# Cross attentions of a fused decoder: pairs of heads on TensorE, three score banks, a shared bank pair for front units and tail

## The chip, the cores and the metric

One core of one Trainium2 chip runs the whole program. The metric is the device time of one execution in microseconds (us), lower is better. The core's engines are TensorE (PE; PEld is its weight load), VectorE (DVE), ScalarE (ACT), GpSimd (POOL) and SyncE (SP, which issues the DMAs). Each runs its own list of instructions in order; they meet through semaphores.

## The reference

Two decoder layers for 16 sequences of 112 tokens with 256 features, in fp32. Each layer has a self attention, a cross attention over 375 context tokens and a feed-forward part, each followed by a residual and a layernorm. The change touches the two cross attentions only (the kernel's stages cross0 and cross1, one function):

```python
Q = split_heads(x @ W_q); K = split_heads(ctx @ W_k); V = split_heads(ctx @ W_v)  # 16 heads of 16
scores = einsum('bhqd,bhkd->bhqk', Q, K) / sqrt(16)      # 112 x 375 a head
scores = where(mask == 0, -1e9, scores)
X = einsum('bhqk,bhkd->bhqd', softmax(scores), V)
x = layernorm(x + merge_heads(X) @ W_o)
```

## The kernel before, in words

`stage_cross_attention` (L395) treats one sequence (a "batch") after another, 16 in each of the two stages; batches 1 to 12 run in a loop of two, the rest are written out (`over_batches`, L475). Within a batch 16 places i = 0..15 follow each other, one a head, and each engine has its own hand-written list of what it does at which place.

For a head h:
- TensorE, `scores` (L685): one matmul, 96 stacked rows, 376 keys, into one of two PSUM banks (h % 2); waits for the maximum of h - 2, which read that bank.
- VectorE, `maximum` (L889): adds the mask, scales, and takes the minimum of the negated scores (L893).
- ScalarE, `exponent` (L799): exponent and row sum (L803), into one of 8 buffers.
- TensorE, `turn` (L694), three places later (TL = 3): three 112 x 125 transposes (L699) into one of two banks; waits for the exponent of h and for the evacuation of h - 2.
- `evacuate`: even heads VectorE (L900), odd heads ScalarE (L809), both at three places' lag (EL = 3).
- TensorE, `values` (L703), for four heads: 24 small matmuls (L712) into bank 6 (OUT).

Two kinds of work are threaded between the heads. The **front units** make the operands of later batches, each in bank u % 2 of the first two: V0, V1, V2 (values, L669, of the next batch; VectorE adds the bias, L871), C0, C1 (context transposes, L664; ScalarE copies, L787), Q (queries, 8 matmuls, L674; ScalarE makes the high part, L791, VectorE the low part, L878), K0, K1 (keys, L681; L796, L883). After them SP stores the parts to DRAM and loads them back stacked, for the batch after the next. The **tail** finishes the batch before, all in bank 7: part 0 ScalarE copies the summed values to osb (L815) and TensorE turns them (L720), VectorE divides by the row sums into otok (L907); part 1 TensorE turns otok (L725), ScalarE copies it to o (L818); part 2 the output product (L731) and VectorE's chain y, variance (L910 to L915); part 3 xn (L919), its transposes (L737) and ScalarE's copy into xt (L821). POOL computes the reciprocal root (L635) and stores x (L637).

The places, by engine (a comment line names the engine; the lists of VectorE and ScalarE are not in the diff except for their banks):

```python
# TensorE: scores(i); turn(i - 3); front; tail; values
TAIL_AT = {6: 0, 8: 1, 10: 2, 14: 3}
FRONT_AT = {2: V0, 4: V1, 6: V2, 7: C0, 8: C1, 10: Q, 12: K0, 14: K1}
VALUES_AT, VALUES_OF_LAST = {8: 0, 12: 1}, {0: 2, 4: 3}
# ScalarE: tail 0; evacuate(i - 3) at even i; exponent(i); front; tail 1, 2
TAIL_AT = {5: 0, 9: 1, 15: 2}
FRONT_AT = {7: C0, 8: C1, 10: Q, 12: K0, 14: K1}
# VectorE: maximum(i); front; tail; evacuate(i - 3) at odd i
TAIL_AT = {7: 0, 11: 1, 13: 2}
FRONT_AT = {5: V0, 6: V1, 7: V2, 11: Q, 13: K0, 15: K1}
```

Each unit on TensorE waits until the reader of the unit two before it is done (`wait_front_read`, L500). The first batch has no tail, the last but one only V units, the last none. Before batch 0 a prologue runs C0, C1, Q, K0, K1 and then all eight units.

## Time and profile before

| | |
|---|---|
| median of 3 runs | 2669.48 us (2666.8 to 2669.84) |
| profiled execution | 2664.71 us, its span 2663.0 us |
| mean granted clock of TensorE over the span | 0.948 |
| PE / PEld / DVE / ACT / POOL busy over the span | 88 / 69 / 65 / 51 / 20 % |
| cross0, all of it | about 150 to 559 us |
| cross1, all of it | about 1305 to 1712 us |
| a middle batch | 306.13 / 13 = 23.55 us |

A matmul's record runs from its start to a modelled end and overlaps the next one's; what a step costs is the time from its start to the start of the next. "[0.40 <-DVE cross_pt L900]" behind a row is the idle time before it and who ended it. An "xN" row merges N instructions.

### The profile page before, as it was taken

The page shows a single profiled execution, that of the slowest core. Times are in us where ns is not written, and L with a number is a line of the kernel's source. Part 1 is how long each engine was busy: PE and PEld are TensorE (multiplying, and loading weights), DVE is VectorE, ACT ScalarE, POOL GpSimd, SP SyncE. Part 2 cuts the span into 40 slices and gives each one's busy share as a digit, 9 for nine tenths or more (in the row PEclk, how much of TensorE's full clock was granted, in tenths as well). Part 3 has the DMA queues.
Part 4 walks back from the last instruction along what each step waited for, and adds up shares of the span by engine and source line. Part 5 has one row for each costly group of instructions (what it writes and reads, how often), then busy time and mean ns, then how long its engine had stood idle before and what let it go on. Part 6 is the DMA issues. An engine that isn't in the chain of part 4 may idle for free. (4 is left out here: it accounts for less than half of the span.)

```text
span 2663.0 us, 51055 instructions
## 1 busy us (share of the span) xinstructions
PE 2346.0 (88%) x15551; PEld 1834.5 (69%) x15551; DVE 1735.1 (65%) x4497; ACT 1357.5 (51%) x3657; POOL 526.4 (20%) x623
## 2 busy tenths in 40 slices
PE   5769999977999968888599999589999999999995
PEld 3547777766999955555377777467777777777762
DVE  1336666763888755666376677546676676767678
ACT  2236666743666515555276666465444444444430
POOL 3010000023000140000100000054343343434321
PEclk8879999978999979999799999889999999999998
DMA  5046655413666420000366665010010100101000
GB/s 161 0 120 130 123 119 119 102 50 112 203 210 208 150 63 1 0 0 0 90 133 122 129 125 124 25 52 17 20 37 2 36 17 22 36 1 37 1 1 28
DMA packets 191015, 194.92 MB, mean 73 GB/s; under 512 B 55457, under 2 KB 182642, under 8 KB 190834
## 3 DMA queue, kind: packets, MB, share of 16 engines
q1 hardware_dynamic: 187762, 185.36, 27.7%
q0 software_dynamic: 3072, 7.34, 0.9%
q8 instruction: 90, 1.47, 0.2%
q14 instruction: 91, 0.75, 0.1%
HBM read 144.23 MB, written 48.43 MB: 72 GB/s over the span
## 5 line engine op out<-in xcount | busy, mean ns | idle before, releaser
L803 ACT ACTIVATE cross_pr<-cross_sc,cross_mn 112x375 f32<-112x375 f32 x512 | 310.5, 607 | 230.6 <-DVE cross_mn L893 229.6
L2317 ACT ACTIVATE switch_vt<-switch_ps,switch_chosen 112x128 f32<-112x128 f32 x1024 | 290.8, 369 | 267.0 <-PE switch_ps L105 256.5
L2391 DVE SCALAR_TENSOR_TENSOR all_x<-switch_ps,switch_go,all_x 112x256 f32<-112x256 f32 x512 | 245.6, 480 | 219.7 <-PE switch_ps L105 214.4
L893 DVE CUSTOM_DVE_ANT_0 cross_sc<-cross_ps,cross_masked 112x375 f32<-112x375 f32 x512 | 273.0, 543 | 176.4 <-PE cross_ps L691 155.3
L699 PE MATMUL cross_ps<-all_ident,cross_pr 112*125 112x112 f32 x1536 | 255.4, 275 | 23.6 <-DVE cross_pt L900 22.0
L699 PEld LDWEIGHTS cross_ps<-all_ident,cross_pr 112*125 112x125 f32 x1536 | 233.0, 189 | 45.3 <-DVE cross_pt L900 27.8
L2182 POOL TENSOR_TENSOR switch_v_halves<-switch_vt 112x512 f32<-112x512 f32 x128 | 164.8, 1287 | 484.3 <-ACT switch_vt L2317 484.1
L2391 DVE SCALAR_TENSOR_TENSOR switchgates_x_odd<-switch_ps,switch_go,switchgates_x_odd 112x256 f32<-112x256 f32 x512 | 243.2, 475 | 0.0
L691 PE MATMUL cross_ps<-cross_k,cross_q 96*112 96x376 f32 x512 | 222.0, 434 | 14.2 <-DMA cross_k<-cross_k_dram 11.1
L103 PE MATMUL switch_ps<-switch_ow,switch_cth 128*112 128x512 f32 x512 | 208.8, 408 | 12.5 <-DVE switchgates_x_odd L2391 12.1
L103 PE MATMUL switch_ps<-switch_vw,switchgates_xh 128*112 128x512 f32 x512 | 208.0, 406 | 7.9 <-DVE switch_vw L2376 7.9
L104 PE MATMUL switch_ps<-switch_vw,switchgates_xh 128*112 128x512 f32 x512 | 202.7, 396 | 0.0
L105 PE MATMUL switch_ps<-switch_vw,switchgates_xl 128*112 128x512 f32 x512 | 202.6, 396 | 0.0
L105 PE MATMUL switch_ps<-switch_ow,switch_ctl 128*112 128x512 f32 x512 | 201.6, 394 | 0.0
L104 PE MATMUL switch_ps<-switch_ow,switch_cth 128*112 128x512 f32 x512 | 201.5, 394 | 0.0
L635 POOL TENSOR_TENSOR cross_rstd<-cross_var,cross_half 112x1 f32<-112x1 f32 x32 | 17.4, 543 | 633.2 <-DVE cross_var L915 633.2
L103 PEld LDWEIGHTS switch_ps<-switch_ow,switch_cth 128*112 128x112 f32 x512 | 89.3, 174 | 70.1 <-DVE switchgates_x_odd L2391 44.7
L103 PE MATMUL experts_ps<-experts_xh,experts_w 128*128 128x256 f32 (+1 forms) x400 | 126.1, 315 | 12.2 <-ACT experts_h L1776 5.5
L900 DVE COPY cross_pt<-cross_ps 125x336 f32<-125x336 f32 x256 | 128.2, 501 | 1.6 <-PE cross_ps L699 1.5
L1776 ACT ACTIVATE experts_h<-experts_ps,experts_b1c 128x256 f32<-128x256 f32 x168 | 79.9, 475 | 86.5 <-PE experts_ps L105 83.8
L2185 POOL TENSOR_TENSOR switch_v_quarters<-switch_v_halves 112x256 f32<-112x256 f32 x128 | 122.0, 953 | 10.1
L103 PE MATMUL experts_ps<-experts_hh,experts_w 128*128 128x256 f32 (+1 forms) x400 | 122.5, 306 | 0.9 <-issue 0.6
(352 smaller groups left out, 5482.0 us busy)
## 6 DMA issues: line engine op xcount, KB each, us to landing
experts_w_raw<-in_L_ffn_w_dram SPq DMA_DIRECT2D x42, 1024.0 KB, 5.2
cross_k<-cross_k_dram SPq DMA_DIRECT2D x96, 375.0 KB, 8.0
cross_k_dram<-cross_ks SPq DMA_DIRECT2D x32, 750.0 KB, 4.6
cross_cx_raw<-in_ctx_dram SPq DMA_DIRECT2D x32, 375.0 KB
cross_q<-cross_q_dram SPq DMA_DIRECT2D x192, 56.0 KB, 4.4
switch_raw<-in_L_ffn_v_w_dram SPq DMA_DIRECT2D x16, 512.0 KB
switch_raw<-in_L_ffn_o_w_dram SPq DMA_DIRECT2D x8, 1024.0 KB, 5.5
cross_q_dram<-cross_qs SPq DMA_DIRECT2D x32, 224.0 KB, 3.6
```

The source lines that it names most:

```text
L103: nc.tensor.matmul(out, w[0], x[0], start=first, stop=False)
L104: nc.tensor.matmul(out, w[0], x[1], start=False, stop=False)
L105: return nc.tensor.matmul(out, w[1], x[0], start=False, stop=last)
L691: nc.tensor.matmul(ps[0:T, SCORES + h % 2, 0:KEYS], q[parity][:, h // 2, h % 2, :], kk[parity][:, h // 2, :], start=True, stop=True).then_ ...
L699: last = nc.tensor.transpose(ps[0:KP, TURNED + h % 2, t * T:(t + 1) * T], pr[:, h % NB, t * KP:(t + 1) * KP], ident[0:T, 0:T])
L803: nc.scalar.activation(pr[:, h % NB, :], sc[:, h % NB, :], ACT.Exp, bias=mn[parity][:, h:h + 1], scale=-1.0, accum_out=rs[parity][:, h:h + ...
L893: nc.vector.tensor_tensor_reduce(out=sc[:, h % NB, :], in0=ps[0:T, SCORES + h % 2, 0:S2], in1=mask_of[:], scale=-0.25, scalar=3e38, op0=AL ...
L900: nc.vector.tensor_copy(pt[:, h % NB, :], ps[0:KP, TURNED + h % 2, 0:KT * T]).then_inc(pt_dve, 1)
L2182: pool.tensor_tensor(v_halves[:], vt[:, b % 2, 0:E // 2, :], vt[:, b % 2, E // 2:E, :], ALU.add)\
L2185: pool.tensor_tensor(v_quarters[:], v_halves[:, 0:E // 4, :], v_halves[:, E // 4:E // 2, :], ALU.add)\
L2317: last = nc.scalar.activation(vt[:, b % 2, n * EH + e, :], ps[0:T, VALUES + n, e * PW:(e + 1) * PW], ACT.Copy, scale=chosen[parity][:, b, ...
L2391: nc.vector.scalar_tensor_tensor(out=total[:, b, :], in0=ps[0:T, OUTPUTS + n % 2, i * D:(i + 1) * D], scalar=go[:, b, e:e + 1], in1=total[ ...
```

## The change

On TensorE the places are taken in pairs: scores of i and i + 1, then turnings i - 3 and i - 2, and then for each place its tail part, its front unit and its values, in that order. C1, Q, K0 and K1 go one place later (9, 11, 13, 15), tail part 0 one place earlier (5). The scores have three banks (2, 3, 4), in the order 0, 1, 2, ... with bank 1 again for head 15; turned heads use banks 5 and 6, the values bank 7. The tail no longer has a bank of its own: parts 0 and 3 use front bank 0, parts 1 and 2 front bank 1. Front bank 0 holds V0, C0, C1, Q; bank 1 holds V1, V2, K0, K1. So the waits of TensorE are new: V0 for Q's reader, V1 for K1's, V2 for V1's, K1 for K0's, C1 for C0's, Q for C1's, C0 for V0's and for otok, K0 for V2's and for the variance, tail part 0 for V0's, part 1 for V2's, part 3 for Q's. The lists of VectorE, ScalarE, POOL and SP keep their order; only bank numbers change there.

```diff
@@ -439,7 +439,9 @@
         rstd = s.sb("rstd", [T, 1])
         xn = s.sb("xn", [T, D])
         ps = s.banks("ps", 8)
-        FRONT, SCORES, TURNED, OUT, TAIL = 0, 2, 4, 6, 7
+        FRONT, SCORES, TURNED, OUT = 0, 2, 5, 7
+        SCORE_BANKS = (0, 1, 2, 0, 1, 2, 0, 1, 2, 0, 1, 2, 0, 1, 2, 1)
+        TAIL_BANK = (0, 1, 1, 0)
 
         dve_passed, sp_passed, pool_passed = s.sem("dve_passed"), s.sem("sp_passed"), s.sem("pool_passed")
         w_loaded, const_loaded, w_turned, w_ready = (s.sem(n) for n in ("w_loaded", "const_loaded", "w_turned", "w_ready"))
@@ -486,7 +488,10 @@
             return {"last": (), "last but one": (V0, V1, V2)}.get(kind, tuple(range(UNITS)))
 
         def bank_of(u):
-            return (FIRST_UNITS + u) % 2
+            return {V0: 0, V1: 1, V2: 1, C0: 0, C1: 0, Q: 0, K0: 1, K1: 1}[u]
+
+        def score_bank(h):
+            return SCORES + SCORE_BANKS[h % H]
 
         def done_count(g, u):
             return g * UNITS + FIRST_UNITS + u + 1
@@ -498,12 +503,6 @@
             return g * DVE_UNITS + FIRST_DVE + DVE_ORDER[u]
 
         def wait_front_read(engine, g, u):
-            if u < 0:
-                g, u = g - 1, u + UNITS
-            if isinstance(g, int) and g < 0 and u < C0:
-                return
-            if isinstance(g, int) and g < -1:
-                return
             if u in (C0, C1):
                 engine.wait_ge(f_act, act_count(g, u))
             else:
@@ -652,10 +651,26 @@
                     last.then_inc(w_turned, 1)
             pe.wait_ge(w_ready, sum(transposed))
 
-            def front(g, parity, u):
+            def front(g, parity, u, tails=True):
+
 
                 bank = ps[:, FRONT + bank_of(u), :]
-                wait_front_read(pe, g, u - 2)
+                if u in (V0, V1):
+                    wait_front_read(pe, g - 1, Q if u == V0 else K1)
+                elif u in (V2, K1):
+                    wait_front_read(pe, g, u - 1)
+                elif u in (C1, Q):
+                    wait_front_read(pe, g, u - 1)
+                elif isinstance(g, int) and g < 0:
+                    pass
+                elif u == C0:
+                    wait_front_read(pe, g, V0)
+                    if tails:
+                        wait(pe, otok_ready, g - 1)
+                elif u == K0:
+                    wait_front_read(pe, g, V2)
+                    if tails:
+                        wait(pe, var_ready, g - 1)
                 if u in (C0, C1):
                     c = u - C0
                     if u == C0:
@@ -687,8 +702,9 @@
                     wait_front_read(pe, b, V2)
                     pe.wait_ge(q_stacked, (b + 1) * Q_PARTS * 16)
                     pe.wait_ge(k_stacked, (b + 1) * K_PARTS * 16)
-                wait(pe, s_max, b * H + h - 1)
-                nc.tensor.matmul(ps[0:T, SCORES + h % 2, 0:KEYS], q[parity][:, h // 2, h % 2, :],
+                taken = max((i for i in range(h - H, h) if score_bank(i) == score_bank(h)))
+                wait(pe, s_max, b * H + taken + 1)
+                nc.tensor.matmul(ps[0:T, score_bank(h), 0:KEYS], q[parity][:, h // 2, h % 2, :],
                                  kk[parity][:, h // 2, :], start=True, stop=True).then_inc(s_done, 1)
 
             def turn(b, h):
@@ -713,55 +729,66 @@
                                                 pt[:, h % NB, t * T:(t + 1) * T], start=t == 0, stop=t == KT - 1)
                 last.then_inc(pv_done, 1)
 
-            def tail(b, part):
+            def tail(b, part, units=()):
+
+                bank = ps[:, FRONT + TAIL_BANK[part], :]
                 if part == 0:
+                    if V0 in units:
+                        wait_front_read(pe, b + 2, V0)
                     pe.wait_ge(o_read, b + 1)
                     for g in range(4):
-                        last = nc.tensor.transpose(ps[0:T, TAIL, g * P:(g + 1) * P], osb[:, g * T:(g + 1) * T], ident[:])
+                        last = nc.tensor.transpose(bank[0:T, g * P:(g + 1) * P], osb[:, g * T:(g + 1) * T], ident[:])
                     last.then_inc(t1_done, 1)
                 elif part == 1:
+                    if V2 in units:
+                        wait_front_read(pe, b + 2, V2)
                     pe.wait_ge(otok_ready, b + 1)
                     for k in range(DC):
-                        last = nc.tensor.transpose(ps[:, TAIL, k * T:(k + 1) * T],
+                        last = nc.tensor.transpose(bank[:, k * T:(k + 1) * T],
                                                    otok[:, k * 8:(k + 1) * 8, :].rearrange("p a b -> p (a b)"), ident[0:T, 0:T])
                     last.then_inc(t2_done, 1)
                 elif part == 2:
                     pe.wait_ge(o_ready, b + 1)
                     for k in range(DC):
-                        last = nc.tensor.matmul(ps[0:T, TAIL, 0:D], o[:, k, :], w[OW][:, k, :],
+                        last = nc.tensor.matmul(bank[0:T, 0:D], o[:, k, :], w[OW][:, k, :],
                                                 start=k == 0, stop=k == DC - 1)
                     last.then_inc(y_done, 1)
                 else:
+                    if Q in units:
+                        wait_front_read(pe, b + 2, Q)
                     pe.wait_ge(xn_ready, b + 1)
                     for k in range(DC):
-                        last = nc.tensor.transpose(ps[:, TAIL, k * T:(k + 1) * T], xn[:, k * P:(k + 1) * P], ident[0:T, 0:T])
+                        last = nc.tensor.transpose(bank[:, k * T:(k + 1) * T], xn[:, k * P:(k + 1) * P], ident[0:T, 0:T])
                     last.then_inc(xt_done, 1)
 
-            TAIL_AT = {6: 0, 8: 1, 10: 2, 14: 3}
-            FRONT_AT = {2: V0, 4: V1, 6: V2, 7: C0, 8: C1, 10: Q, 12: K0, 14: K1}
+            TAIL_AT = {5: 0, 8: 1, 10: 2, 14: 3}
+            FRONT_AT = {2: V0, 4: V1, 6: V2, 7: C0, 9: C1, 11: Q, 13: K0, 15: K1}
 
             def batch(b, parity, kind):
                 first, units = kind == "first", units_of(kind)
-                for i in range(H):
-                    scores(b, parity, i)
-                    if i >= TL:
-                        turn(b, i - TL)
-                    elif not first:
-                        turn(b - 1, i - TL + H)
-                    if FRONT_AT.get(i) in units:
-                        u = FRONT_AT[i]
-                        front(b + 1, 1 - parity if u in (V0, V1, V2) else parity, u)
-                    if not first and i in TAIL_AT:
-                        tail(b - 1, TAIL_AT[i])
-                    if i in VALUES_AT:
-                        values(b, parity, VALUES_AT[i])
-                    elif i in VALUES_OF_LAST and not first:
-                        values(b - 1, 1 - parity, VALUES_OF_LAST[i])
+                for pair in range(0, H, 2):
+                    for i in (pair, pair + 1):
+                        scores(b, parity, i)
+                    for i in (pair, pair + 1):
+                        if i >= TL:
+                            turn(b, i - TL)
+                        elif not first:
+                            turn(b - 1, i - TL + H)
+                    for i in (pair, pair + 1):
+                        if not first and i in TAIL_AT:
+                            tail(b - 1, TAIL_AT[i], units)
+                        if FRONT_AT.get(i) in units:
+                            u = FRONT_AT[i]
+                            front(b + 1, 1 - parity if u in (V0, V1, V2) else parity, u, not first)
+                        if i in VALUES_AT:
+                            values(b, parity, VALUES_AT[i])
+                        elif i in VALUES_OF_LAST and not first:
+                            values(b - 1, 1 - parity, VALUES_OF_LAST[i])
 
             for u in (C0, C1, Q, K0, K1):
-                front(-1, 0, u)
+                front(-1, 0, u, False)
             for u in range(UNITS):
-                front(0, 0 if u in (V0, V1, V2) else 1, u)
+                front(0, 0 if u in (V0, V1, V2) else 1, u, False)
             over_batches(pe, batch)
             for h in range(H - TL, H):
                 turn(B - 1, h)
@@ -815,10 +842,10 @@
                     nc.scalar.copy(osb[:], ps[:, OUT, 0:4 * T]).then_inc(o_read, 1)
                 elif part == 1:
                     act.wait_ge(t2_done, b + 1)
-                    nc.scalar.copy(o[:].rearrange("p a b -> p (a b)"), ps[:, TAIL, 0:DC * T]).then_inc(o_ready, 1)
+                    nc.scalar.copy(o[:].rearrange("p a b -> p (a b)"), ps[:, FRONT + TAIL_BANK[1], 0:DC * T]).then_inc(o_ready, 1)
                 else:
                     act.wait_ge(xt_done, b + 1)
-                    nc.scalar.copy(xt[:, :, ds(b * T, T)], ps[:, TAIL, 0:DC * T].rearrange("p (a b) -> p a b", a=DC))\
+                    nc.scalar.copy(xt[:, :, ds(b * T, T)], ps[:, FRONT + TAIL_BANK[3], 0:DC * T].rearrange("p (a b) -> p a b", a=DC))\
                         .then_inc(xt_ready, 1)
 
             TAIL_AT = {5: 0, 9: 1, 15: 2}
@@ -890,7 +917,7 @@
 
                 wait_apart(dve, dve_passed, (s_done, b * H + h + 1), (exped, b * H + h - NB + 1))
                 mask_of = masked[parity if mask_by_batch else 0]
-                nc.vector.tensor_tensor_reduce(out=sc[:, h % NB, :], in0=ps[0:T, SCORES + h % 2, 0:S2], in1=mask_of[:],
+                nc.vector.tensor_tensor_reduce(out=sc[:, h % NB, :], in0=ps[0:T, score_bank(h), 0:S2], in1=mask_of[:],
                                                scale=-0.25, scalar=3e38, op0=ALU.add, op1=ALU.min,
                                                accum_out=mn[parity][:, h:h + 1]).then_inc(s_max, 1)
 
@@ -904,12 +931,12 @@
                     dve.wait_ge(exped, b * H + H)
                     ch.link(nc.vector.reciprocal(ri[:], rs[parity][:]))
                     dve.wait_ge(t1_done, b + 1)
-                    nc.vector.tensor_tensor(otok[:], ps[0:T, TAIL, :].rearrange("p (h e) -> p h e", e=32)[:, :, 0:HD],
+                    nc.vector.tensor_tensor(otok[:], ps[0:T, FRONT + TAIL_BANK[0], :].rearrange("p (h e) -> p h e", e=32)[:, :, 0:HD],
                                             ri[:].unsqueeze(2).broadcast_to([T, H, HD]), ALU.mult).then_inc(otok_ready, 1)
                 elif part == 1:
                     ch.link(nc.vector.tensor_add(y[:].unsqueeze(1), x[:, ds(b, 1), :], o_bias[:].unsqueeze(1)))
                     dve.wait_ge(y_done, b + 1)
-                    ch.link(nc.vector.tensor_add(y[:], ps[0:T, TAIL, 0:D], y[:]))
+                    ch.link(nc.vector.tensor_add(y[:], ps[0:T, FRONT + TAIL_BANK[2], 0:D], y[:]))
                     ch.link(nc.vector.bn_stats(st[:], y[:]), dve_passed)
                     ch.link(nc.vector.bn_aggr(mv[:], st[:]))
                     nc.vector.tensor_scalar_add(var[:], mv[:, 1:2], EPS).then_inc(var_ready, 1)
```

## Rows read from the trace of the kernel before

**Rows 1.** Windows, batches 1 to 13 of both stages: stretch, length, busy (count), PEclk, DMA, GB/s
```profile
199.39:505.52 306.13, 286.79 (x2681) 222.15 (x2680) 214.33 (x716) 210.56 (x637) 12.23 (x26) 1.00 0.60 121
1346.30:1652.61 306.31, 286.83 (x2681) 222.09 (x2680) 214.39 (x716) 210.64 (x637) 18.96 (x39) 1.00 0.59 123
```

**Rows 2.** Waits of batches 1 to 13, cross0: who <- whom: total us, times, longest
```profile
DVE cross_sc L893 <- PE cross_ps L691: 59.4, 54, 1.7
...
PE cross_ps L699 <- DVE cross_pt L900: 8.2, 21, 0.5
```

**Rows 3.** Timeline of TensorE in batch 7, cross0: start, duration, engine, line, names, shapes
```profile
344.23 1.04 PE L669 MATMUL cross_ps<-cross_w,cross_cx 128*125 128x256 f32 x4
...
344.92 0.52 PE L691 MATMUL cross_ps<-cross_k,cross_q 96*112 96x376 f32 x1
...
345.52 0.41 PE L691 MATMUL cross_ps<-cross_k,cross_q 96*112 96x376 f32 x1
...
345.77 0.48 PE L699 MATMUL cross_ps<-all_ident,cross_pr 112*125 112x112 f32 x3
...
346.09 1.04 PE L669 MATMUL cross_ps<-cross_w,cross_cx 128*125 128x256 f32 x4
...
347.06 0.78 PE L712 MATMUL cross_ps<-cross_pt,cross_v 125*32 125x112 f32 x24
...
347.77 0.43 PE L691 MATMUL cross_ps<-cross_k,cross_q 96*112 96x376 f32 x1
```

**Rows 4.** Timeline of TensorE, the same batch, later
```profile
350.39 0.60 PE L720 MATMUL cross_ps<-all_ident,cross_osb 128*112 128x128 f32 x4
...
352.33 0.54 PE L664 MATMUL cross_ps<-all_ident,cross_cx_raw 125*128 125x125 f32 x3
...
355.08 1.06 PE L674 MATMUL cross_ps<-all_xt,cross_w 128*128 x8
...
356.23 1.12 PE L731 MATMUL cross_ps<-cross_w,cross_o 128*112 128x256 f32 x4
...
358.16 1.44 PE L681 MATMUL cross_ps<-cross_cx,cross_w 128*128 128x375 f32 x4
...
361.07 0.58 PE L699 MATMUL cross_ps<-all_ident,cross_pr 112*125 112x112 f32 x3 [0.40 <-DVE cross_pt L900]
```

**Rows 5.** Timeline of VectorE, the same stretch
```profile
342.11 0.61 DVE L883 SCALAR_TENSOR_TENSOR cross_ks<-cross_ps,cross_qk_bias,cross_ks 128x375 fp32r<-128x375 f32 x1 [0.68 <-ACT cross_ks L796]
...
345.72 0.55 DVE L893 CUSTOM_DVE_ANT_0 cross_sc<-cross_ps,cross_masked 112x375 f32<-112x375 f32 x1 [0.77 <-PE cross_ps L691]
...
351.86 0.42 DVE L871 TENSOR_TENSOR cross_v<-cross_ps,cross_v_bias 125x256 f32<-125x256 f32 x1
...
352.47 0.42 DVE L907 TENSOR_TENSOR cross_otok<-cross_ps,cross_ri 112x256 f32<-112x256 f32 x1
...
358.22 0.57 DVE L878 SCALAR_TENSOR_TENSOR cross_qs<-cross_ps,cross_qk_bias,cross_qs 128x112 fp32r<-128x112 f32 x2
...
358.70 0.41 DVE L910 TENSOR_TENSOR cross_y<-all_x,cross_o_bias 112x256 f32<-112x256 f32 x1
...
360.50 0.51 DVE L900 COPY cross_pt<-cross_ps 125x336 f32<-125x336 f32 x1
```

**Rows 6.** Timeline of ScalarE, the same stretch
```profile
341.52 0.55 ACT L796 ACTIVATE cross_ks<-cross_ps,cross_qk_bias 128x375 fp32r<-128x375 f32 x1
...
347.91 0.52 ACT L815 COPY cross_osb<-cross_ps 128x448 f32<-128x448 f32 x1
...
352.58 0.45 ACT L787 COPY cross_cx<-cross_ps 128x375 f32<-128x375 f32 x1
...
355.25 0.61 ACT L803 ACTIVATE cross_pr<-cross_sc,cross_mn 112x375 f32<-112x375 f32 x1 [0.38 <-DVE cross_mn L893]
...
355.85 0.32 ACT L818 COPY cross_o<-cross_ps 128x224 f32<-128x224 f32 x1
...
357.01 0.59 ACT L791 ACTIVATE cross_qs<-cross_ps,cross_qk_bias 128x112 fp32r<-128x112 f32 x2
```

**Rows 7.** Windows, the end of cross0, where no front units are left
```profile
530.00:555.00 25.00, 17.55 (x201) 13.16 (x200) 14.43 (x50) 13.33 (x42) 1.88 (x4) 0.92 0.01 2
```

## The prediction

> **What bounds the kernel now.** I read the windows view of the two stretches of middle batches first, because only these two stages contain the changed lines. Each stretch runs from the first scores of batch 1 to those of batch 14: 13 batches in 306.13 and 306.31 us, so 23.55 us a batch, and TensorE is busy 286.79 us of it [rows 1]. That is 22.06 us of work a batch and 1.49 us idle. VectorE (214.33) and ScalarE (210.56) have about 7 us a batch to spare. So TensorE is the bound, but it is an engine that walks a fixed list, and each item may wait for VectorE or ScalarE, which walk fixed lists of their own. The waits view says which wait ends late: of TensorE's the longest is the turning's, held by VectorE's evacuation L900, 8.2 us over the 13 batches; VectorE in turn waits 59.4 us for scores that stand late in TensorE's list [rows 2]. Then the timeline: it shows that the list of before works because between a unit and the turning that depends on its readers there is other TensorE work. The queries' product starts at 355.08, the turning that waits behind its readers only at 361.07 [rows 4], 6.0 us later, and of those TensorE lost 0.4 us.
>
> The Trainium skill, "Perfetto Trace Analysis", Identifying the Most-Contended Engine, would have TensorE's distance from its limit judged by the busy share of weight loads, not of matmuls. That is 222.15 of 306.13 us here, 17.1 us a batch [rows 1], so by it 6.5 us a batch are to be had and not 1.5; what that makes of the gain stands with the rivals.
>
> **The change, part by part.** The instructions are the same. What changes is TensorE's list and the banks.
>
> *Pairs.* Scores of two heads, then turnings of two. From the start of one step to the next, rows 3 show scores to turning 0.25 us, turning to what follows 0.32 (345.77 to 346.09), a V unit to scores 0.69, a V unit to values 0.97, values 0.71. Scores directly after scores occur nowhere in the trace. The nearest row is scores to turning, 0.25 with another operand type behind it; for the lower end, a turning's three matmuls follow each other at 0.11 for a record of 0.27, and in that proportion the scores' 0.41 gives 0.16. I take 0.18, nearer the matmuls of one kind, with ends of 0.16 and 0.25. A pair is then 0.18 + 0.25 + 0.32 + 0.32 = 1.07 us against about 1.0 now (0.24 + 0.25 a head): +0.5 us a batch on TensorE, hidden where it waits anyway.
>
> *Three score banks.* Scores of head h then wait for the maximum of h-3 instead of h-2. TensorE's wait for a maximum is not the one that rows 2 name as its longest, and in rows 3 and 4 scores follow turnings without idle time, so I give it nothing. The bank pattern's exceptions (head 15 after 13, head 1 after 15) ask for maxima that are done by then.
>
> *The tail in the front units' banks, and what moved past what.* VectorE's and ScalarE's lists are unchanged: VectorE still does V1's bias at place 6, V2's and the tail's first part at 7, the queries' low part and the whole layernorm chain at 11 before it evacuates head 8, the keys at 13 and 15 before heads 10 and 12. But TensorE's turnings 8, 10, 12, 14 (lag 3) wait for those evacuations, and the front units now stand behind both turnings of a pair. So where 4 to 5 us of other TensorE work lay between a unit and the turning that depends on it, one pair lies there now. I walked one middle batch round, with 0.2 us from a TensorE end to its reader (scores at 344.92 + 0.52 to the maximum at 345.72 is 0.28; values at 347.06 + 0.78 to osb at 347.91 is 0.07 [rows 3, 5, 6]) and 0.05 from a VectorE or ScalarE end to TensorE:
>
> 1. C1 to the output product. C1 0.54 [rows 4], pickup 0.2, ScalarE's copy 0.45, exponent 9 0.60, copy of o 0.32, 0.05 [rows 6] = 2.16. TensorE has 0.25 + 1.07 of its own: idle 0.8.
> 2. Output product 0.69 (as a V unit). Then the queries' product Q.
> 3. Q to turning 10: Q 1.06, pickup 0.2, ScalarE 0.59 [rows 6], 0.05, VectorE's low part 0.48 (358.22 to 358.70), the y chain 1.80 (358.70 to 360.50), evacuation of head 8 0.51, 0.05 [rows 5] = 4.74. TensorE has Q's 0.9 and scores 12, 13, turning 9, 0.75: idle 3.1.
> 4. Turning 10 and values 1: 1.1.
> 5. K0 to turning 12: K0 1.44 [rows 4], 0.2, ScalarE and its handover 0.59 (341.52 to 342.11), VectorE 0.61, xn 0.41 (as L910, the same size), evacuation 0.51, 0.05 = 3.81; own work 2.0, idle 1.8.
> 6. Turning 12 and tail part 3: 0.57.
> 7. K1 to turning 14: as 5 without xn, 3.40; idle 1.4.
> 8. Turning 14, values 2, pair, V0, pair, V1, values 3: 0.32 + 0.71 + 1.07 + 0.69 + 1.07 + 0.97 + 0.78 = 5.61. No wait in it.
> 9. Tail part 0 now comes right behind values 3 and needs ScalarE's copy of them: 0.1 + 0.52 + 0.05 = 0.67, all idle; its four transposes 0.4 [rows 4, 6].
> 10. Scores 6 to C0, which now waits for otok, because they share bank 0: maximum 6 starts 0.80 later, takes 0.55, V1's bias 0.42, 0.05, V2 1.04 and pickup 0.25, V2's bias and reciprocal 0.61 (351.86 to 352.47), otok 0.42, 0.05 [rows 3, 5] = 4.19; own work 1.8, idle 2.4.
> 11. C0 0.25, pair 1.07, tail part 1 0.35, values 0 0.80 = 2.45, and C1 again.
>
> The sum is 29.8 us. VectorE starts an instruction up to 0.09 before the record of the last one ends (358.22 + 0.57 against 358.70), about five such steps, so I take 29.4. Against 23.55 that is +5.85 us a batch, and 26 middle batches: +152 us. The cover that each wait would need is in the list: step 3 lacks 3.1 us, step 10 2.4, step 5 1.8, step 7 1.4.
>
> *The ends.* Batch 0 has no tail: steps 5 and 7 and a shorter 3 remain, estimate +1.5 us. Batches 14 and 15 have no Q and K: +0.5. In the prologue C0, C1 and Q now follow each other through one bank, each behind the last one's reader, and K1 behind K0's; the first scores wait for the keys' DMA after K1, so about 2 us. Together 4 a stage (ends 0 and 8), 8 us. The DMA queues issue the same transfers in the same order; their share is 0.60 of the stretch [rows 1], and a longer batch gives them more room. SP waits for the low parts of Q and K as before: a batch lies between them and the scores that need them, so nothing is added. POOL waits for var and xn only, and is busy 1 us a batch [rows 1].
>
> Against the profiled execution's 2664.7 us the sum is 2664.7 + 152 + 8 = 2825 us. That execution was 4.8 us under the median of the runs shown (0.2%, and 0.2% is also about what a measurement of this kernel can tell from no change).
>
> **Rivals.**
> - *The clock falls as well.* In the stretches of rows 1 the granted clock is 1.00, the 2.4 GHz level. At the stage's end, where no front units fill TensorE, it is busy 17.55 of 25 us, and the clock is 0.92 [rows 7]. The change brings a similar share, about 22 of 29.4. If it takes 0.92 throughout, 16% of the time is spent at 1.2 GHz, and the 15.9 us of the walk that are TensorE's own grow by 2.5: 26 x 2.5 = 66, giving 2891. Against it: there most of the rest is transposes, while K, Q and V units remain here. The Trainium skill, "TensorE: Matmul & The Clock Gate", HAM oscillation, says that waits between bursts of matmuls let the clock fall back in each turn of a loop; the end-of-stage row agrees with its direction.
> - *Milder.* The engines are not in step as I walked it: ScalarE or VectorE is further ahead at the start of a chain, and six tenths of the added idle time are overlapped. Then +2.2 a batch, 2664.7 + 26 x 2.2 = 2722.
> - *Faster.* The pairs do what pairs are good for: exponents of a pair run beside the other pair's scores, and TensorE no longer waits. Its place is turning 10: it decides if the evacuation of head 8 is done before TensorE gets there, 1.65 us after Q's start. All 1.49 us idle a batch saved gives 2664.7 - 39 = 2626. For it: rows 2 name just this wait as the one to remove. Against it: the chain behind Q is 4.74 us and no part of it got shorter. By the skill's reading above (weight loads as the limit) it would be 26 x 6.5 = 169 us and 2496; the row of before, where steps follow each other without a gap at the times that I used, speaks against that.
> - *No change.* Waits only change places within a batch whose TensorE work is given: 2665. It needs all added idle time to stand where there was as much before; the 0.4 at 361.07 against 3.1 says no.
>
> **How the numbers follow.** Forecast (all chains stand end to end, clock 1.00) 0.72; clock as well 0.13; milder 0.06; faster 0.06; no change 0.03. The forecast's own bounds: pickups of 0.07 for 0.2 and 0.16 for scores to scores take 1.0 off a batch (2799); 0.25 for scores to scores and 0.7 for a loop's turn every second batch add 1.2 (2856). With ends of 0 and 16 us, and half a microsecond a batch for waits that I walked wrong, 2780 to 2880. The range must also take in most of the clock case and some of the milder one: 2750 to 2900. Slower by over 0.2%: 0.72 + 0.13 + 0.06 = 0.91; within 0.03; faster 0.06.
>
> **What would show it.** In the changed profile: a middle batch of 29 to 30 us; TensorE busy about 21.5 of it; TensorE's wait of L699 for VectorE's cross_pt (L900) up to 3 us long, some 6 us a batch and 80 us over the 13 batches, where it has 8.2 now [rows 2]; C0's transposes (L664 before) waiting for otok by 2 us; tail 0's for osb by 0.6; the maxima (L893) no longer waiting 1.6 us on scores beside Q. I am wrong if turning 10 follows turning 9 without a gap, or if the batch stays under 25 us. If the batch is over 31 us, the clock row decides whether the rival has it.

## The result and the profile after

| | before | after |
|---|---|---|
| median (runs) | 2669.66 us (4) | 2871.08 us (4; 2867.6 to 2879.54) |
| ratio | | 1.0761, 95% interval 1.0734 to 1.0788 |
| profiled execution, span | 2663.0 us | 2865.9 us |
| a middle batch, mean | 23.55 us | 30.85 us |
| a middle batch at full clock | 23.55 us | 29.6 us |

The change is 7.6% slower. I forecast 2825 us, range 2750 to 2900. The windows view of the 13 middle batches in both stages, as in [rows 1]:

```profile
206.27:610.36 404.09, 302.64 (x2681) 239.69 (x2679) 217.14 (x715) 220.36 (x636) 12.24 (x26) 0.93 0.45 92
1456.59:1854.50 397.91, 294.30 (x2681) 234.50 (x2679) 217.35 (x715) 220.02 (x636) 19.07 (x40) 0.95 0.46 95
```

The two stretches grew by 97.96 and 91.60 us, 189.6 of the span's 202.9. VectorE and ScalarE run the same instructions as before and are busy about 3 and 10 us longer a stretch. TensorE's matmul time rose only because some of it ran at the slower clock (0.93 and 0.95 granted): in a batch at full clock it is 21.61 us, as the clock rows below show, against 22.06 before. The waits view of the changed kernel in the second stage (L715 is the turning, L679 the context transposes, L740 tail part 0, L753 the output product):

```profile
PE cross_ps L715 <- DVE cross_pt L927: 66.2, 39, 3.0
...
DVE cross_sc L920 <- PE cross_ps L707: 42.2, 60, 0.9
...
PE cross_ps L679 <- DVE cross_otok L934: 15.9, 12, 1.3
...
PE cross_ps L740 <- ACT cross_osb L842: 9.7, 13, 0.7
...
PE cross_ps L753 <- ACT cross_o L845: 5.4, 13, 0.4
```

TensorE's wait for VectorE's evacuation is 66.2 us here and 64.2 in the first stage, up to 3.0 us at a time; it was 8.2 us and 0.5 [rows 2]. VectorE's idle time for scores fell instead, from 59.4 [rows 2] to 46.0 in the same stage. TensorE's timeline over one walk's round at full clock, from C1 on:

```profile
1594.86 0.54 PE L679 MATMUL cross_ps<-all_ident,cross_cx_raw 125*128 125x125 f32 x3
...
1596.80 1.12 PE L753 MATMUL cross_ps<-cross_wraw,cross_o 128*112 128x256 f32 x4 [0.41 <-ACT cross_o L845]
1597.75 1.04 PE L689 MATMUL cross_ps<-all_xt,cross_wraw 128*128 x8
...
1598.98 0.48 PE L715 MATMUL cross_ps<-all_ident,cross_pr 112*125 112x112 f32 x3
1602.40 0.58 PE L715 MATMUL cross_ps<-all_ident,cross_pr 112*125 112x112 f32 x3 [2.95 <-DVE cross_pt L927]
1602.91 0.78 PE L728 MATMUL cross_ps<-cross_pt,cross_v 125*32 125x112 f32 x24
1603.62 1.53 PE L696 MATMUL cross_ps<-cross_cx,cross_wraw 128*128 128x375 f32 x4
...
1605.33 0.48 PE L715 MATMUL cross_ps<-all_ident,cross_pr 112*125 112x112 f32 x3
1607.20 0.58 PE L715 MATMUL cross_ps<-all_ident,cross_pr 112*125 112x112 f32 x3 [1.39 <-DVE cross_pt L927]
...
1607.81 1.44 PE L696 MATMUL cross_ps<-cross_cx,cross_wraw 128*128 128x375 f32 x4
...
1610.97 0.47 PE L715 MATMUL cross_ps<-all_ident,cross_pr 112*125 112x112 f32 x2 [1.06 <-DVE cross_pt L927]
```

and its end, from values 3 and tail part 0 to the next C1:

```profile
1616.11 0.78 PE L728 MATMUL cross_ps<-cross_pt,cross_v 125*32 125x112 f32 x24
1617.63 0.62 PE L740 MATMUL cross_ps<-all_ident,cross_osb 128*112 128x128 f32 x4 [0.74 <-ACT cross_osb L842]
1618.01 0.59 PE L707 MATMUL cross_ps<-cross_k,cross_q 96*112 96x376 f32 x2
...
1622.12 0.54 PE L679 MATMUL cross_ps<-all_ident,cross_cx_raw 125*128 125x125 f32 x3 [1.33 <-DVE cross_otok L934]
...
1624.48 0.33 PE L679 MATMUL cross_ps<-all_ident,cross_cx_raw 125*128 125x125 f32 x1
```

The reader should look at 1598.98 to 1602.40: turning 9, then 2.95 us without work, until VectorE has evacuated head 8. The same at 1607.20 (1.39, head 10) and 1610.97 (1.06, head 12).

The clock, in a window that ends with a batch at full clock (it starts 0.3 us ahead of that batch), in the next batch, and in the stretch right behind the latter's wait at turning 10:

```profile
1578.90:1608.80 29.90, 21.61 (x209) 17.37 (x208) 16.73 (x55) 16.90 (x49) 1.75 (x4) 1.00 0.49 98
1608.80:1640.71 31.91, 24.17 (x208) 19.05 (x207) 16.69 (x55) 17.02 (x49) 1.46 (x3) 0.89 0.44 92
1632.00:1638.50 6.50, 6.28 (x36) 4.30 (x36) 1.68 (x6) 2.02 (x6) 0.14 (x1) 0.50 0.00 0
```

TensorE's timeline in that stretch:

```profile
1628.59 0.48 PE L715 MATMUL cross_ps<-all_ident,cross_pr 112*125 112x112 f32 x3
1632.02 0.97 PE L715 MATMUL cross_ps<-all_ident,cross_pr 112*125 112x112 f32 x3 [2.95 <-DVE cross_pt L927]
...
1634.20 2.87 PE L696 MATMUL cross_ps<-cross_cx,cross_wraw 128*128 128x375 f32 x4
```

The second batch is 2.3 us longer (31.91 against 29.60 us, from first scores to first scores), and all of it lies behind turning 10, where TensorE's clock stood at 0.50, the 1.2 GHz level, after 2.95 us of idle time. Of the 26 middle batches 6 ran at full clock throughout (29.6 us), 12 were 0.8 to 1.4 us longer and 8 were 1.8 to 3.8 us longer. The trace has 21 stretches at 1.2 GHz in them; 20 begin between 0.8 us before and 1.8 us after the end of turning 10's wait, the other one right behind C0's wait of 1.32 us.

### The profile page after: what moved, and what is told of

Read it like the earlier page. It is cut to its first block and busy times, and to the rows that moved or that the text cites. A ratio compares the mean times of both kernels' runs of the same rounds, so it can differ in the third digit from the quotient of the medians.

```text
span 2865.9 us, 51195 instructions
## 1 busy us (share of the span) xinstructions
PE 2368.5 (83%) x15551; PEld 1863.6 (65%) x15551; DVE 1742.0 (61%) x4497; ACT 1377.0 (48%) x3657; POOL 527.8 (18%) x623
## 3 DMA queue, kind: packets, MB, share of 16 engines
q1 hardware_dynamic: 187762, 185.36, 25.7%
## 5 line engine op out<-in xcount | busy, mean ns | idle before, releaser
L715 PE MATMUL cross_ps<-all_ident,cross_pr 112*125 112x112 f32 x1536 | 242.8, 285 | 148.1 <-DVE cross_pt L927 144.9
L715 PEld LDWEIGHTS cross_ps<-all_ident,cross_pr 112*125 112x125 f32 x1536 | 222.6, 197 | 168.4 <-DVE cross_pt L927 134.0
L920 DVE CUSTOM_DVE_ANT_0 cross_sc<-cross_ps,cross_masked 112x375 f32<-112x375 f32 x512 | 261.7, 545 | 109.2 <-PE cross_ps L707 105.1
L105 PE MATMUL switch_ps<-switch_vw,switchgates_xl 128*112 128x512 f32 x512 | 202.9, 396 | 0.0
L707 PE MATMUL cross_ps<-cross_k,cross_q 96*112 96x376 f32 x512 | 178.6, 431 | 4.5 <-DMA cross_k<-cross_k_dram 3.8
L836 ACT COPY cross_pt<-cross_ps 125x336 f32<-125x336 f32 x256 | 112.6, 440 | 61.9 <-PE cross_ps L715 60.9
L910 DVE SCALAR_TENSOR_TENSOR cross_ks<-cross_ps,cross_qk_bias,cross_ks 128x375 fp32r<-128x375 f32 x64 | 39.0, 609 | 166.2 <-ACT cross_ks L823 166.2
```

The lines of the kernel that those rows point to most:

```text
L105: return nc.tensor.matmul(out, w[1], x[0], start=False, stop=last)
L707: nc.tensor.matmul(ps[0:T, score_bank(h), 0:KEYS], q[parity][:, h // 2, h % 2, :], kk[parity][:, h // 2, :], start=True, stop=True).then_i ...
L715: last = nc.tensor.transpose(ps[0:KP, TURNED + h % 2, t * T:(t + 1) * T], pr[:, h % NB, t * KP:(t + 1) * KP], ident[0:T, 0:T])
L920: nc.vector.tensor_tensor_reduce(out=sc[:, h % NB, :], in0=ps[0:T, score_bank(h), 0:S2], in1=mask_of[:], scale=-0.25, scalar=3e38, op0=ALU ...
```

## Experiments

All are timed beside the kernel before, and each ratio is to the kernel before; "batch" is the distance of the first scores of middle batches. Line numbers shift with the edits: the turning is L699 in kernels made from before, L715 or L711 in those from after.

### Parts of the change alone

**e1, the pairs alone.** The kernel before, its `batch` on TensorE taken in pairs. Everything else is kept, also the order at a place (front unit, then tail part, then values), where the change has the tail part first:

```diff
-                for i in range(H):
-                    scores(b, parity, i)
+                for pair in range(0, H, 2):
+                    for i in (pair, pair + 1):
+                        scores(b, parity, i)
...
```

> The kernel before, with TensorE's places taken in pairs (two scores, two turnings, then front units, tail, values of both places), but with its own places for the units, two score banks and the tail's own bank. Lists theory (units stand behind the turnings of a pair while VectorE evacuates after its own unit): waits at turning 10 of 2.3 us, 12 of 1.1, 14 of 1.2 come, small waits of before go; a middle batch of 24 to 25 us, 2685 to 2710 us. Bank theory (the loss comes from the tail sharing the front units' banks): as before, 2665 to 2675 us. Pair theory (two scores and two turnings in a row are costly by themselves): most of the loss is there, 2830 us or more.

Measured: 2715.9 us, ratio 1.0166 (1.0149 to 1.0183), 6 us above the range of the lists theory and far from the others. Batch 24.9 us at full clock, 25.4 in the mean (granted 0.97). TensorE's timeline around Q:

```profile
1646.40 1.06 PE L674 MATMUL cross_ps<-all_xt,cross_wraw 128*128 x8
1647.30 1.03 PE L731 MATMUL cross_ps<-cross_wraw,cross_o 128*112 128x256 f32 x4
...
1648.51 0.48 PE L699 MATMUL cross_ps<-all_ident,cross_pr 112*125 112x112 f32 x3
1651.07 0.58 PE L699 MATMUL cross_ps<-all_ident,cross_pr 112*125 112x112 f32 x3 [2.08 <-DVE cross_pt L903]
...
1654.97 0.58 PE L699 MATMUL cross_ps<-all_ident,cross_pr 112*125 112x112 f32 x3 [0.49 <-DVE cross_pt L903]
```

Q (L674) stands ahead of the output product (L731) here. The output product therefore covers 0.9 us of the chain behind Q, and the wait is 2.08 us, not 2.95; at turning 12 it is 0.49. So pairs over an unfitted VectorE list cost 1.3 us a batch at full clock, and 46 us in all, a quarter of the loss.

**e5, the shared banks undone.** On the changed kernel:

```diff
-        FRONT, SCORES, TURNED, OUT = 0, 2, 5, 7
-        SCORE_BANKS = (0, 1, 2, 0, 1, 2, 0, 1, 2, 0, 1, 2, 0, 1, 2, 1)
-        TAIL_BANK = (0, 1, 1, 0)
+        FRONT, SCORES, TURNED, OUT = 0, 2, 4, 6
+        SCORE_BANKS = (0, 1) * 8
+        TAIL_BANK = (7, 7, 7, 7)
```

and without the waits of C0, K0 and tail parts 0, 1, 3 that only the shared banks need.

> The changed kernel with the tail back in a bank of its own and two score banks instead of three, so C0 no longer waits for otok, K0 not for the variance, and tail parts not for front units' readers. Places, pairs and all other lists as changed. Lists theory: only step 10 of the walk shrinks (2.1 us idle before C0 gone, 0.4 back at tail part 1), the waits at turnings 10, 12, 14 stay at 3.0, 1.7, 1.4: 27.7 us a batch, 2826 us, 2810 to 2840. Bank theory: most of the loss goes, under 2740 us. Two score banks instead of three cost nothing, as every maximum that they ask for is done: a wait of scores (L707) for a maximum would show otherwise.

Measured: 2859.83 us, ratio 1.0701 (1.0676 to 1.0726), above the range of the lists theory. The batch is 28.8 us at full clock, but only 2 of the 26 ran so (6 in the change); with a stretch at 1.2 GHz in the others (granted 0.93 and 0.94) the mean is 30.3 us against 30.85:

```profile
1681.59 0.49 PE L675 MATMUL cross_ps<-all_ident,cross_cx_raw 125*128 125x125 f32 x3
...
1683.30 0.58 PE L711 MATMUL cross_ps<-all_ident,cross_pr 112*125 112x112 f32 x3 [0.56 <-DVE cross_pt L917]
...
1692.26 0.58 PE L711 MATMUL cross_ps<-all_ident,cross_pr 112*125 112x112 f32 x3 [2.95 <-DVE cross_pt L917]
```

C0 (L675) starts right after V2, but turning 6 then waits 0.56 us for head 4, which VectorE evacuates behind otok: I had left that out. The banks are worth 0.8 us a batch at full clock, not 1.9; the wait at turning 10 is 2.95 as before. The bank theory falls: it had the time under 2740 us. Two score banks instead of three added no wait of scores for a maximum.

**e6, the pairs undone.** On the changed kernel, `range(0, H, 2)` became `range(H)` and all three `(pair, pair + 1)` became `(pair,)`.

> The changed kernel with TensorE's places taken singly again (scores i, turning i - 3, then tail, front, values of i), but at the changed places and with the changed banks. Lists theory: the later places and the shared banks do most of it; the waits at turnings 10 and 14 shrink to 2.2 and 0.6 us, the one at 12 stays, C0 still waits near 2 us: 28.3 us a batch with fewer clock drops, 2815 to 2835 us. Pair theory: most of the loss goes with the pairs, under 2740 us.

Measured: 2926.65 us, ratio 1.0964 (1.0931 to 1.0997), slower than the changed kernel. Both theories had the sign wrong. The windows view of the second stage's middle batches, then of one of its shorter batches and of the slow stretch in it:

```profile
1488.00:1914.06 426.06, 329.94 (x2680) 263.04 (x2679) 219.19 (x715) 217.19 (x636) 18.99 (x40) 0.85 0.43 89
1589.60:1620.52 30.92, 23.03 (x208) 18.48 (x207) 16.86 (x55) 16.76 (x49) 1.45 (x4) 0.94 0.45 94
1604.10:1607.50 3.40, 3.40 (x36) 2.79 (x34) 1.26 (x5) 1.29 (x4) 0.00 (x0) 0.50 0.52 104
```

From its waits view over the same stretch, the longest of VectorE and of ScalarE:

```profile
DVE cross_sc L920 <- PE cross_ps L707: 132.9, 103, 2.7
ACT cross_pr L830 <- DVE cross_mn L920: 94.0, 88, 2.9
```

From TensorE's timeline of that batch, steps that waited, and values 0 in the slow stretch (0.78 us at full clock):

```profile
1597.87 0.65 PE L740 MATMUL cross_ps<-all_ident,cross_osb 128*112 128x128 f32 x4 [0.91 <-DVE cross_v L898]
...
1599.92 1.13 PE L684 MATMUL cross_ps<-cross_wraw,cross_cx 128*125 128x256 f32 x4 [0.92 <-DVE cross_v L898]
...
1603.24 0.54 PE L679 MATMUL cross_ps<-all_ident,cross_cx_raw 125*128 125x125 f32 x3 [1.71 <-DVE cross_otok L934]
...
1604.64 1.35 PE L728 MATMUL cross_ps<-cross_pt,cross_v 125*32 125x112 f32 x24
...
1615.21 0.58 PE L715 MATMUL cross_ps<-all_ident,cross_pr 112*125 112x112 f32 x3 [2.05 <-DVE cross_pt L927]
```

The wait at turning 10 shrank to 2.05 as expected, but others grew: with single places the scores of i + 1 stand behind whatever i waits for, VectorE's wait for scores is 132.9 us against 42.2, and tail part 0, V2 and C0 wait 0.91, 0.92 and 1.71 where the change has 0.74, 0.42 and 1.33.

None of the 26 middle batches of this run is at full clock throughout; they take 32.9 us in the mean. The batch shown has 3.4 us at the 1.2 GHz level, all of it busy; halved, that gives an estimate of 29.2 us for a batch at full clock, or a little more if waits behind it hid some of the loss. This is about the change's 29.6. So what is slower than the change is in the main the clock, and this run doesn't show that pairs shorten the chain.

### VectorE's list

**e2, evacuate first.** On the changed kernel:

```diff
             FRONT_AT = {5: V0, 6: V1, 7: V2, 11: Q, 13: K0, 15: K1}
+            EARLY = (11, 13, 15)
...
                     maximum(b, parity, i)
+                    if i in EARLY:
+                        evacuate(b, i - EL)
                     if FRONT_AT.get(i) in units:
...
-                    if (i - EL) % 2 == 0:
+                    if (i - EL) % 2 == 0 and i not in EARLY:
```

> The changed kernel, with VectorE evacuating heads 8, 10 and 12 right after the maxima 11, 13 and 15, ahead of its low parts of Q, K0, K1 and the layernorm chain. TensorE's list and banks as changed. Lists theory: the waits at turnings 10, 12 and 14 (6.3 us a batch) go; about 1.7 us come back as a wait of scores 15 for maximum 13 and of the tail's xn; the batch falls by 4.4 us to about 25.2, the clock stays at 1.00: 2725 us, 2700 to 2760. Bank theory: the waits of C0, tail 0 and the output product are what matters, little changes: over 2840 us.

Measured: 2748.11 us, ratio 1.0299 (1.0281 to 1.0316), inside the range of the lists theory. All but two batches take 25.7 to 26.7 us, clock 0.99 and 1.00.

```profile
1571.31 0.81 PE L715 MATMUL cross_ps<-all_ident,cross_pr 112*125 112x112 f32 x6
...
1574.33 1.50 PE L696 MATMUL cross_ps<-cross_cx,cross_wraw 128*128 128x375 f32 x4 [1.50 <-issue]
...
1577.55 0.38 PE L761 MATMUL cross_ps<-all_ident,cross_xn 112*128 112x112 f32 x2 [0.73 <-DVE cross_xn L946]
```

Turnings 9 and 10 (the row of six) run through. Three instructions a batch, moved on one engine, took 123 us of the 201 back: the mean batch fell from 30.85 to 26.55 us, 3.2 us by the chain (29.6 to 26.4 at full clock) and 1.1 by the clock. What was missed of the expected batch is K0 (L696), which shares its bank with the output product and waits 1.50 us (the row says only "issue"; the wait that stands ahead of it in the list is for the layernorm chain's variance, which VectorE finishes 0.11 us before K0 starts: L942, 1574.07 + 0.15); I had not carried that over from the walk, where turning 10's wait hid it.

**e9, units first.** On e5, within a pair the front units, then values, then the tail, instead of tail, front, values place by place.

> As the run with the tail's own bank (28.8 us a batch at full clock), but within a pair TensorE takes the front units first, then values, then tail. Lists theory: the output product (0.95 us) and values 1 (0.8) leave the chain and become cover for the waits at turnings 10 and 12, Q no longer waits for o (0.5): waits at turning 10 of about 2.1 us and at 12 of 0.9; 26.5 us a batch, 2760 us, 2745 to 2790. Rival (the order within a pair does not matter, the pairs and the later places do): over 2830 us.

Measured: 2767.02 us, ratio 1.0386 (1.037 to 1.0402), as expected; batch 26.2 us at full clock, 26.9 in the mean. The order within a pair is worth 2.6 us a batch at full clock: the order decides whether the output product and values 1 stand ahead of a wait, as cover, or between two waits, on the chain.

The ratios of e1, e9, e5 and the change make a ladder (times 2670 us): pairs 44 us, the places moved later (with values ahead of the tail) 59, the tail first within a pair 84, the shared banks 16, together 203. The steps overlap with the clock and depend on their order; no run moved the places alone.

### The clock

**e3, a filler.** On the changed kernel, in middle batches, ahead of turning 10 and behind its wait for the exponent:

```diff
+                if filler:
+                    pe.wait_ge(s_max, b * H + 12)
+                    for _ in range(4):
+                        nc.tensor.matmul(ps[:, score_bank(14), 0:S2], w[KW][:, 0, 0:P], cx[:, 0, :], start=True, stop=True)
```

> The changed kernel, with four more 375-column matmuls (1.25 us, results unused) in middle batches while TensorE waits for the evacuation of head 8, so ahead of turning 10. They lie inside an idle time of 3 us and lengthen no chain. Clock theory (the idle time at turning 10 is what lets the clock fall to 1.2 GHz, and that costs the 2.3 us by which 31.9 us batches exceed 29.6 us ones): granted clock near 1.00 in both stages, batches of 29.6 us, 32 us less in all, 2839 us, 2830 to 2850. Rival (the clock falls by the other waits, or costs nothing since the chains are VectorE's and ScalarE's): 2865 to 2880 us.

Measured: 2843.9 us, ratio 1.0651 (1.0634 to 1.0667), its interval clear of the change's and inside the range of the clock theory. More work, less time: the clock is back at 0.99 and 1.00, and 22 of the 26 middle batches are 29.6 us long or less (the others 31.1 to 31.3). The four matmuls are kept by nobody: their results are overwritten by scores 14. The windows view of the two stages' middle batches, and from the waits view of the second the turning's wait for VectorE, 66.2 us in the change:

```profile
207.35:596.46 389.11, 314.72 (x2785) 245.41 (x2783) 217.28 (x715) 219.34 (x636) 12.23 (x26) 0.99 0.47 96
1446.27:1832.23 385.96, 311.44 (x2784) 242.58 (x2783) 217.39 (x715) 219.25 (x636) 19.09 (x40) 1.00 0.47 98
...
PE cross_ps L719 <- DVE cross_pt L931: 37.1, 39, 1.5
```

The two stretches are 389.11 and 385.96 us against 404.09 and 397.91: 27 us less, the whole gain. So it is in the main the idle time at turning 10 that lets the clock fall, as the 20 of 21 slow stretches of the change say too. It is not that wait alone: the four slow stretches that are left here begin 0.1 to 0.6 us behind C0's wait of 1.33 us.

### A better version

**e4, e7, e8, e11** start from the kernel before. e4 is e2's edit on it; e7 moves the layernorm chain too; e8 also V0 and V1; e11 also tail part 3 on TensorE:

```diff
-            TAIL_AT = {7: 0, 11: 1, 13: 2}
-            FRONT_AT = {5: V0, 6: V1, 7: V2, 11: Q, 13: K0, 15: K1}
+            TAIL_AT = {7: 0, 12: 1, 13: 2}
+            FRONT_AT = {4: V0, 5: V1, 7: V2, 11: Q, 13: K0, 15: K1}
...
-            TAIL_AT = {6: 0, 8: 1, 10: 2, 14: 3}
+            TAIL_AT = {6: 0, 8: 1, 10: 2, 15: 3}
```

> The kernel before, with the same reordering of VectorE's list alone. Lists theory: turning 10's wait of 0.4 to 0.6 us a batch goes, and scores 0 come earlier: 0.6 to 0.9 us a batch, 2645 to 2655 us. Rival (the layernorm chain and the low parts now come 0.5 us later and the wait moves to them): 2665 to 2672 us.

Measured: 2659.15 us, ratio 0.9959 (0.9945 to 0.9972), between the two expected ranges. The wait at turning 10 went, but scores 14 now wait for maximum 12, which stands behind the layernorm chain; TensorE waits 0.73 us there. The batch is 23.05 us.

> The kernel before, VectorE evacuating heads 8, 10, 12 ahead of its units at places 11, 13, 15, and the layernorm chain moved from place 11 to place 12, behind maximum 12. The 0.7 us for which scores 14 wait for maximum 12 in the run with the evacuations alone go: 22.5 us a batch, 2643 us, 2638 to 2652. Rival (maximum 13 and the keys' low part now come late and TensorE waits for xn or exponent 13): 2655 to 2665.

Measured: 2650.09 us, 0.9922 (0.9905 to 0.994): 22.6 us a batch, 0.4 less than e4, near the slow end of the expected range.

> As the run with the chain at place 12, and VectorE takes V0 at place 4 and V1 at 5 instead of 5 and 6, so that V2 (waits for V0's reader, 0.6 us a batch in rows of before) finds its bank free: 0.5 us a batch more, 2630 us, 2624 to 2642. Rival (V0 waits there for the values of the batch before and holds up maximum 5): no gain on the run before.

Measured: 2629.91 us, 0.985 (0.9824 to 0.9875), as expected: V2's wait for V0's reader (4.8 us over twelve batches in e4) is gone, and the batch is 22.0 us.

> The run with V0 and V1 early, single places, and tail part 3 at TensorE's place 15 instead of 14. The 0.7 to 0.9 us a batch for which TensorE waits for xn there are covered by scores 15 and turning 12: 0.6 us a batch, 2614 us, 2608 to 2622. Rival (something else ends then as late): 2622 to 2632.

Measured: 2623.55 us, 0.9844 (0.983 to 0.9857): not told apart from e8, as the rival had it. Over twelve batches TensorE's wait for xn fell from 7.8 to 2.4 us, and scores wait 3.0 us for a maximum instead.

**e10 and e12, pairs on the fitted list.** e10 is e8 with e1's pairs; e12 has V0 and V1 back at VectorE's places 5 and 6.

> VectorE's list of the run with V0 and V1 early (evacuations of heads 8, 10, 12 ahead of the units, layernorm chain at place 12), and TensorE's places in pairs, banks as before. If pairs cost nothing once VectorE's list fits them: 2625 to 2645 us. If the 0.07 us a pair that two scores and two turnings take more, and turnings 9 to 14 still late, show: 2650 to 2690 us.

Measured: 2629.31 us, 0.9866 (0.9851 to 0.9881), as e8 without pairs, though the batch is 22.3 us against 22.0. One wait stood out in the timeline, 0.76 us for the second scores of a pair, behind VectorE's V0.

> The paired kernel with VectorE's fitted list, but V0 and V1 back at VectorE's places 5 and 6. In the paired run VectorE took V0 at place 4, where it waits for the values of the batch before, and maximum 5 stood behind it, so that scores of place 7 came 0.76 us late. With V0 behind maximum 5 that wait goes, and V2 waits for V0's reader no longer than now: 21.7 to 21.9 us a batch, 2615 us, 2608 to 2625. Rival (V2's wait for V0's reader comes back and takes the same): 2625 to 2640.

Measured: 2612.08 us, ratio 0.9777 (0.9763 to 0.979), the fastest version, 2.2% under the kernel before and 9% under the change. It is e7 with pairs and nothing else (2650.09 us), so over this list of VectorE's the pairs save 38 us, where over the list of before they cost 46 (e1). Its windows view:

```profile
201.88:481.71 279.83, 272.17 (x2680) 220.38 (x2679) 214.09 (x715) 220.13 (x636) 12.20 (x26) 1.00 0.65 133
1325.92:1605.83 279.91, 272.19 (x2681) 220.46 (x2679) 213.89 (x715) 219.66 (x636) 18.61 (x40) 1.00 0.65 135
```

and TensorE's timeline from Q on, where turnings 9 and 10 run through into K0:

```profile
1490.83 1.06 PE L674 MATMUL cross_ps<-all_xt,cross_wraw 128*128 x8
1491.72 1.03 PE L731 MATMUL cross_ps<-cross_wraw,cross_o 128*112 128x256 f32 x4
...
1492.94 0.81 PE L699 MATMUL cross_ps<-all_ident,cross_pr 112*125 112x112 f32 x6
1493.58 0.81 PE L681 MATMUL cross_ps<-cross_cx,cross_wraw 128*128 128x375 f32 x2
```

## Why the prediction was right

**Lists out of step: right.** The walk gave 29.8 us and I took 29.4; the batch is 29.62. Step by step, predicted and measured (from the starts in the two timelines): C1 to output product 2.16 / 1.94; to Q 0.69 / 0.95; Q to turning 10 4.74 / 4.65; to K0 1.1 / 1.22; K0 to turning 12 3.81 / 3.58; to K1 0.57 / 0.61; K1 to turning 14 3.40 / 3.16; to the end of values 3 5.61 / 5.92; to tail part 0 0.67 / 0.74; to scores 6 0.4 / 0.38; to C0 4.19 / 4.11; to C1 2.45 / 2.36. At full clock that is 26 x 6.05 = 157 us, against 152. No step is off by more than 0.31 us, but the errors go both ways, and that their sum is 0.2 is in part luck. TensorE's recorded waits are a little shorter than I named (66.2 and 64.2 us against 80 at the turnings, 1.33 against 2 at C0). e2 shows the cause at three of the four places by removal; the fourth, C0's, was removed in e5 and gave 0.8 us, since turning 6 then waits.

**The clock: the term that I left at zero.** The forecast had a granted clock of 1.00, and the case with both had 66 us. It is 189.6 - 157 = 32 us, 1.2 us a batch in the mean, with nothing in 6 batches and up to 3.8 us in one. e3 takes 27 of them back. I read the falling clock from a stretch with the same busy share [rows 7] and gave it 0.13; better evidence for it was in my own walk, a 3 us hole in every batch. So the time lies between the forecast and that rival, and what failed in the forecast is the assumption that the two were alternatives. The median also lies inside the forecast's own bounds (2780 to 2880), but none of their terms is the clock's: without its 32 us the median would be near 2839, so that part of the agreement is luck. The Trainium skill, "TensorE: Matmul & The Clock Gate", HAM oscillation, describes a wait, there for a DMA, between bursts of matmuls that drops the clock in each turn of a loop. The row of 1632.00 to 1638.50 (granted 0.50) agrees with its direction; here the wait is for another engine, and 20 of 26 turns are hit, not each.

**Ends:** 202.9 - 189.6 = 13.3 us against 8. The first scores of cross0 come 3.2 us later (183.83 against 180.64), batch 0 takes 22.44 against 18.75 us there and 19.86 against 18.83 in cross1.

The 46 us between the forecast's 2825 and the median of 2871 are thus 5 of the walk, 32 of the clock and 5 of the ends; the last 3.5 are the distance of the changed kernel's median from its profiled execution (2867.6).

**Scores after scores:** two in a row have a record of 0.58 to 0.59 us, one has 0.41: 0.17 to 0.18 from start to start, as taken.

**The rivals.** "Faster" failed at its own place: turning 10 was reached 3 us before the evacuation. Yet the pairs do what it said once VectorE's list fits (e12 against e7: 21.5 us a batch against 22.6). Its bound by TensorE's idle time, 1.49 us a batch, was too small: e12's batch is 21.5 us, 2.0 less. TensorE's busy time by records fell too, from 286.8 to 272.2 us a stretch, with the same instructions and clock; I take it that a record covers part of a wait (a turning that waited has a record of 0.58 us, others 0.48), but no run isolates that. The reading by weight loads (17.1 us a batch) was not reached. "Milder" and "no change" have nothing for them.

**What I had wrong beside it:** that the pairs have a price of their own. They cost 46 us over the lists of before (e1) and save 38 over a fitted one (e12 against e7); over the changed places undoing them made the kernel 56 us slower (e6), in the main by the clock.

## What to carry to other kernels

Where several engines follow hand-written lists, a place in one list is a promise to the others: before moving a unit, find the consumer that waits for the last thing that the other engine does behind that unit, and sum the chain up to it against the work left between them. Moving the small evacuation ahead of the long chain on the engine that has time to spare took back 123 us, the change of banks 11. Walk one steady round with start-to-start times from the trace; and where the walk shows a hole of about 3 us, as here, in TensorE's work, price the clock too.

## What was not expected of the hardware

Four extra matmuls of 375 columns in every middle batch made the program 27 us faster, because the clock stayed at 2.4 GHz (0.99 and 1.00 instead of 0.93 and 0.95). What the clock costs differs from variant to variant, by the mean batch against one at full clock: 1.2 us in the change, 1.5 in e5, where it took back a third of what a shorter chain gave, and some 3.7 in e6 (0.85 in the second stage), by the estimate of 29.2 us. It does not follow the longest wait alone: in e6 that is 2.1 us and in the change 3.0. Open is how much idle time it takes; no run varied the filler or put it elsewhere.
